# Null keys of the first wide attention: weights kept by token, scores scaled on GpSimd, the residual sum a tick later

## The reference, cut to what matters

```python
nkv = null_kv.reshape(HEADS, NUM_NULL_KV, 2, DIM_HEAD)
k = jnp.concatenate([nk, k], axis=2); v = jnp.concatenate([nv, v], axis=2)
q = _l2norm(q) * q_scale;  k = _l2norm(k) * k_scale
sim = jnp.einsum('bhid,bhjd->bhij', q, k) * ATTN_SCALE      # ATTN_SCALE = 8
sim = sim + dist * slopes                                    # alibi; then the causal mask
attn = jax.nn.softmax(sim, axis=-1)
out = jnp.einsum('bhij,bhjd->bhid', attn, v)
return out.transpose(0, 2, 1, 3).reshape(b, n, HEADS * DIM_HEAD) @ w_out
```

## Time and profile before

| | |
|---|---|
| median of 3 runs | 2622.32 us |
| the profiled execution | 2621.87 us |
| its span, first to last instruction | 2620.2 us |
| TensorE matmul busy | 2392.0 us (91%) |
| VectorE / ScalarE / GpSimd busy | 1722.9 (66%) / 1481.1 (57%) / 1605.7 us (61%) |
| mean granted TensorE clock | 0.968 |
| GpSimd's power in `pool_rstd` (L2593) | 256 times, mean 589 ns |
| GpSimd's power in the norm (L912) | 64 times, mean 2934 ns |

### The profile page before, as it was taken

One profiled execution on the slowest core, in us unless ns is written; L12 is line 12 of the kernel. 1 busy time (PEld: TensorE's weight loads), 2 busy tenths in 40 slices (PEclk: granted clock), 3 DMA queues, 4 the chain that ended last, 5 costly groups with the idle time before them and its releaser, 6 DMA issues. The chain is left out here.

```text
span 2620.2 us, 62757 instructions
## 1 busy us (share of the span) xinstructions
PE 2392.0 (91%) x24121; PEld 1873.6 (72%) x24121; DVE 1722.9 (66%) x4520; ACT 1481.1 (57%) x3071; POOL 1605.7 (61%) x2517
## 2 busy tenths in 40 slices
PE   4999999999998778888999999999999958789897
PEld 3888888888887556556777787787777748555555
DVE  4667677677775657785544467777777622477776
ACT  3666666666654457765444366666666523366665
POOL 4777777778786644443433267777777721566664
PEclk8999999999999969999999999999999979799999
DMA  3692000000000010000000000000000036000000
GB/s 115 205 331 84 2 2 2 2 2 2 2 2 1 1 53 2 2 2 1 23 1 1 3 2 6 6 4 6 6 6 4 6 116 190 17 8 10 8 4 33
DMA packets 23257, 83.12 MB, mean 32 GB/s; under 512 B 4113, under 2 KB 11026, under 8 KB 21938
## 3 DMA queue, kind: packets, MB, share of 16 engines
q1 hardware_dynamic: 19810, 71.90, 8.5%
q0 software_dynamic: 3152, 7.21, 0.9%
HBM read 71.89 MB, written 46.79 MB: 45 GB/s over the span
## 5 line engine op out<-in xcount | busy, mean ns | idle before, releaser
L891 POOL TENSOR_TENSOR XR<-XR,T 128x256 f32<-128x256 f32 x512 | 376.2, 735 | 151.9 <-DVE T L770 121.7
L645 ACT ACTIVATE P<-ps 128x384 f32<-128x384 f32 (+1 forms) x512 | 250.6, 542 | 177.4 <-PE ps L2575 176.0
L2575 PE MATMUL ps<-P,V 128*64 128x256 f32 (+3 forms) x4096 | 334.6, 348 | 7.0 <-DVE O L1396 5.2
L1380 DVE TENSOR_REDUCE bm<-ps 128x3 f32<-128x384 f32 x512 | 260.1, 550 | 100.5 <-PE ps L2575 99.8
L2575 PEld LDWEIGHTS ps<-P,V 128*64 128x64 f32 (+1 forms) x4096 | 186.3, 124 | 126.7 <-issue 32.2
L1305 ACT ACTIVATE P<-ps 128x768 f32<-128x768 f32 x256 | 207.7, 811 | 101.9 <-PE ps L2575 99.7
L781 DVE TENSOR_REDUCE sm<-ps 128x2 f32<-128x512 f32 (+1 forms) x256 | 130.8, 553 | 179.1 <-PE ps L2575 178.9
L1480 POOL TENSOR_SCALAR_AFFINE_SELECT P<-P 128x512 f32<-128x512 f32 x256 | 162.6, 635 | 124.3 <-ACT P L1305 122.4
L904 POOL TENSOR_TENSOR PS<-P 128x256 f32<-128x256 f32 x256 | 181.5, 734 | 69.5 <-ACT P L645 69.1
L2575 PE MATMUL ps<-mk,identb 128*128 128x256 bf16 (+1 forms) x1024 | 205.5, 296 | 17.2 <-DVE bm L1380 15.4
L912 POOL TENSOR_TENSOR ss<-ss,nhalf 128x16 f32<-128x16 f32 x64 | 187.8, 2934 | 5.3
(11 more groups left out here) (323 smaller groups left out, 7152.0 us busy)
## 6 DMA issues: line engine op xcount, KB each, us to landing
rows_i<-in_zero SPq DMA_DIRECT2D x16, 1208.0 KB, 32.0
rows_o<-in_zero SPq DMA_DIRECT2D x16, 1208.0 KB, 81.6
w<-in_m_w SPq DMA_DIRECT2D x23, 578.0 KB, 4.0
zt<-rows_i SPq DMA_DIRECT2D x23, 128.0 KB, 3.1
rows_o<-yo POOLq DMA_DIRECT2D x23, 128.0 KB, 3.7
stg<-in_t_w SPq DMA_DIRECT2D x11, 256.0 KB, 2.7
XR<-in_x SPq DMA_DIRECT2D x4, 512.0 KB, 8.4
out<-XR SPq DMA_DIRECT2D x8, 256.0 KB, 2.0
```

The costliest lines, as they stand in the source:

```text
L645: e.activation(self.P[at % 6][:, :], K.ps.ap("st", s, g, h)[:, 0:self.w], ACT.Exp, bias=0.0, scale=1.0 if kind == 0 else 0.125).then_inc(K ...
L891: p = po.e.tensor_tensor(x, x, self.T[g % 2][:, par, pr], ALU.add)
L1380: e.tensor_reduce(bm[:, h, :], K.ps.ap("mx", s, g, h)[:, 0:384].rearrange("p (a c) -> p a c", c=128), X, ALU.max, negate=True).then_inc(K. ...
L2575: return self.te.matmul(o, l, r, start=start, stop=True, skip_group_check=True)
```

## The change

Stage 0 alone is changed. The null keys' part leaves the products of each unit. GpSimd scales the null scores and adds the bias, right behind the norm (`pool_null`). It later adds the two exponentials of a head (`sm[:, 48:56]`), which VectorE adds to the transposed row sums before the reciprocal. In tick 22 GpSimd multiplies the exponentials by rs into pn, which is now one tile of 128 tokens by 64 for a whole sequence ("shared"). A new item "null" of each sequence starts when its last unit has ended: k = 0, TensorE transposes pn and ScalarE copies it into pnT; k = 1, TensorE multiplies pnT by nvw, "nul"; k = 2, VectorE adds nul to XR, after GpSimd's last sum. nvw, the null values times w_out, is made once, by eight matmuls and two copies in unit (0, 0). A unit has 24 ticks; its residual sum moves to the tick after "out", last in that tick (rank 7). Preps come last in a tick on VectorE. SP stages kb first and nvs, now one piece, last.

```diff
-            first, last, unit = 8, 9, 23
+            first, last, unit = 8, 9, 24
...
+            if kind == 0:
+                items.append((16 * b + first + 12 + unit, 2, "null", (b,), 3))
...
+        self.dve_order = [w for w in ticks(items, self.dve_rank) if not self.is_early(*w)]
...
     def done(self, b):
-        return self.summed, 4 * b + 4
+        return self.K.ps.read("nul", self.s, b) if self.kind == 0 else (self.summed, 4 * b + 4)
...
# rank
+        if name == "null":
+            return 3 if k == 0 else 2
# pool_rank
+        if name == "unit" and k == self.tk["out"] + 1:
+            return 7
+    def dve_rank(self, name, k):
+        return 6 if self.kind == 0 and name == "prep" else self.rank(name, k)
...
+    def pe_nvw(self, pe):
+        K, n = self.K, self.nvs_at
+        ps = K.ps.take(pe, self.G, "nvw")
+        K.staged(pe, n)
+        for j in range(8):
+            p = pe.e.matmul(ps[0:64, 0:128], K.stg[n % 2][:, 64 * j:64 * j + 64], K.wO[:, 128 * j:128 * j + 128],
+                            start=j == 0, stop=j == 7)
+        p.then_inc(K.ps.full_of("nvw"), 1)
+    def pe_null(self, pe, b, k):
+        K, s = self.K, self.s
+        if k == 0:
+            ps = K.ps.take(pe, self.G, "pnT", s, b)
+            pe.wait_ge(self.shared, 4 * b + 4)
+            K.tr(ps[0:64, 0:128], self.pn[b % 2][:, :]).then_inc(K.ps.full_of("pnT", s, b), 1)
+        if k == 1:
+            ps = K.ps.take(pe, self.G, "nul", s, b)
+            pe.wait_ge(self.nvs_in, 1)
+            pe.wait_ge(*K.ps.read("nvw"))
+            pe.wait_ge(*K.ps.read("pnT", s, b))
+            K.acc(ps[:, 0:256], self.pnT[b % 2][:, :], self.nvw[:, :], start=True).then_inc(K.ps.full_of("nul", s, b), 1)
...
# pe_unit, step mT
-            if kind == 0:
-                pe.wait_ge(self.pnull, g + 1)
-                for i in range(2):
-                    p = K.tr(ps[0:96, 256 + 128 * i:384 + 128 * i], fv(self.pn[g % 2][:, i, :]))
...
# pe_pv
-        if kind == 0:
-            pe.wait_ge(self.nvs_in, 4)
-            pe.wait_ge(*K.ps.read("mT", s, g))
-            for pr in range(2):
-                c = 256 * u + 128 * pr
-                K.acc(pv[:, 256 * pr:256 * pr + 256], self.nvs[:, 0, c:c + 128], self.pnT[g % 2][:, :], start=pr == 0)
-            K.acc(sm[:, 0:256], self.nvo[:, 4 * u:4 * u + 4, :].rearrange("p h c -> p (h c)"), self.pnT[g % 2][:, :],
-                  start=True)
...
# act_unit, step mT
-                i = e.activation(self.pnT[g % 2][:, :], ps[0:96, 256:512], ACT.Copy)
...
# dve
+            elif name == "null":
+                if k == 2:
+                    b = a[0]
+                    xs = K.XR[:, 2 * b:2 * b + 2, :].rearrange("p t c -> p (t c)")
+                    dv.wait_ge(self.summed, 4 * b + 4)
+                    dv.wait_ge(*K.ps.filled("nul", self.s, b))
+                    e.tensor_tensor(xs, K.ps.ap("nul", self.s, b)[:, 0:256], xs, ALU.add).then_inc(
+                        K.ps.out_of("nul", self.s, b), 1)
...
# dve_unit, step sT (kind 0)
+                if g >= 2:
+                    dv.wait_ge(self.shared, g - 1)
+                dv.wait_ge(self.pnull, g + 1)
...
+                dv.after(dv.step(e.tensor_tensor(rs[:, :], sums, self.sm[g % 4][:, 48:56], ALU.add)))
+            e.reciprocal(rs[:, :], rs[:, :] if kind == 0 else sums).then_inc(K.ps.out_of("sT", s, g), 1)
...
# dve_null: the four products and sums go, the reduction stays
+        dv.wait_ge(self.scored, g + 1)
...
# pool
-                if k == self.tk["out"] + (1 if self.kind == 2 else 0):
+                if k == self.tk["out"] + 1:
                     self.pool_sum(po, *a)
+    def pool_null(self, po, g):
...
+        po.wait_ge(*K.ps.read("sn", s, b))
+        if g >= 4:
+            po.wait_ge(self.rec, g - 3)
+        po.after(po.step(e.tensor_tensor(sn, snr, rq, ALU.mult)))
+        e.tensor_tensor(sn, sn, nb, ALU.add).then_inc(self.scored, 1)
...
# pool_unit: k == 3 ends with self.pool_null(po, g); k == 12 and k == 22:
+            ex = sm[:, 32:48].rearrange("p (a n) -> p a n", n=2)
+            e.tensor_tensor(sm[:, 48:56], ex[:, :, 0], ex[:, :, 1], ALU.add).then_inc(self.pnull, 1)
+        if k == self.tk["out"]:
...
+            po.wait_ge(*K.ps.read("sT", s, g))
+            e.tensor_tensor(
+                self.pn[b % 2][:, :].rearrange("p (t h n) -> p t h n", t=2, n=2)[:, :, 4 * u:4 * u + 4, :], ex,
+                self.rs[g % 2][:, :].rearrange("p (t h) -> p t h", t=2).unsqueeze(3).to_broadcast([128, 2, 4, 2]),
+                ALU.mult).then_inc(self.shared, 1)
```

More of the change, by code:

```diff
@@ L182, in __init__ @@
             self.sn = [sb(f"sn{s}_{i}", [128, 64], F32) for i in range(2)]
[L183 to L186, removed]
+            self.pn = [sb(f"pn{s}_{i}", [128, 64], F32) for i in range(2)]
+            self.pnT = [sb(f"pnT{s}_{i}", [64, 128], F32) for i in range(2)]
+            self.nvw = sb(f"nvw{s}", [64, 256], F32)
             self.on = sb(f"on{s}", [128, 128], F32R)
@@ L502, in pe_pv @@
                     p = K.acc(pv[64 * par:64 * par + 64, 256 * pr + q:256 * pr + q + w], V[:, kt, 2 * pr + par, :],
-                              P[2 * pr + par][:, c:c + w], start=kind == 2 and kt == 0 and pr == 0)
+                              P[2 * pr + par][:, c:c + w], start=kt == 0 and pr == 0)
         p.then_inc(K.ps.full_of("pv", s, g), 1)
@@ L507, in pe_pv @@
                 for h in range(4):
-                    p = K.acc(sm[32 * h:32 * h + 32, q:q + w], self.one[:, 0:32], P[h][:, c:c + w])
+                    p = K.acc(sm[32 * h:32 * h + 32, q:q + w], self.one[:, 0:32], P[h][:, c:c + w], start=kt == 0)
             p.then_inc(K.ps.full_of("sm", s, g), 1)
@@ L545, in act @@
                 a[0].act(ac, a[1], k)
+            elif name == "null":
+                if k == 0:
+                    b = a[0]
+                    if b >= 2:
+                        ac.wait_ge(*self.K.ps.filled("nul", self.s, b - 2))
+                    ac.wait_ge(*self.K.ps.filled("pnT", self.s, b))
+                    ac.e.activation(self.pnT[b % 2][:, :], self.K.ps.ap("pnT", self.s, b)[0:64, 0:128], ACT.Copy).then_inc(
+                        self.K.ps.out_of("pnT", self.s, b), 1)
             elif name == "unit":
@@ L548, in act @@
                     self.act_kb(ac)
+                if self.kind == 0 and a == (0, 0) and k == 8:
+                    self.act_nvw(ac)
                 self.act_unit(ac, *a, k)
@@ L565, in act_kb, with act_nvw @@
             e.activation(o, i, ACT.Copy).then_inc(self.kb_in, 1)
+    def act_nvw(self, ac):
+        K = self.K
+        ac.wait_ge(self.nv_zero, 1)
+        ac.wait_ge(*K.ps.filled("nvw"))
+        for t in range(2):
+            r = slice(32 * t, 32 * t + 32)
+            i = ac.e.activation(self.nvw[r, 128 * t:128 * t + 128], K.ps.ap("nvw")[r, 0:128], ACT.Copy)
+            i.then_inc(*((K.ps.out_of("nvw"), 1) if t else (self.nvs_in, 1)))
     def act_prep(self, ac, b, k):
@@ L670, in dve @@
                 K.ps.out_of("beff"), 1)
-        for name, a, k in self.order:
+        for name, a, k in self.dve_order:
             if name == "prep":
@@ L848, in pool @@
         if self.kind == 0:
-            for pn in self.pn:
-                e.memset(fv(pn[:, :, :]), 0.0).then_inc(K.pn_in, 1)
+            e.memset(self.nvw[:, :], 0.0).then_inc(self.nv_zero, 1)
         for name, a, k in self.pool_order:
@@ L935, in sp @@
         if self.kind == 0:
-            for n, (a, b) in enumerate(((0, 512), (512, 1024), (1024, 1040))):
-                n += self.nvs_at
-                K.sp_stage(sp, n, K.stg[n % 2][0:96, 0:b - a], K.t["nvs"][:, a:b])
             for c in range(5):
@@ L941, in sp @@
                 K.sp_stage(sp, n, K.stg[n % 2][:, 0:w], K.t["kb0"][:, 512 * c:512 * c + w])
+            K.sp_stage(sp, self.nvs_at, K.stg[self.nvs_at % 2][:, :], K.t["nvs"])
         else:
@@ L2840, in lay_out @@
     t["blk"] = blk
-    nv, no = np.zeros((96, 16, 64), f), np.zeros((96, 16), f)
+    nv = np.zeros((2, 64, 8, 2, 32), f)
     for h in range(16):
         for n in range(2):
-            for r in range(3):
-                at = 32 * r + 4 * (h % 2) + 2 * (h % 4 // 2) + n
-                nv[at, h], no[at, h] = nkv[h, n, 1], 1
-    t["nvs"] = np.concatenate([nv.reshape(96, 1024), no], 1)
+            nv[h % 2, :, h // 2, :, 2 * h + n] = nkv[h, n, 1][:, None]
+    t["nvs"] = nv.reshape(128, 512)
     t["wqT"] = np.ascontiguousarray(i["L0_attn_w_q"].T.reshape(8, 128, 128).transpose(1, 0, 2).reshape(128, 1024))
```

90 lines of the change are left out of this document (34 added, 56 removed).

## The result

The changed kernel takes 2667.39 us, median of 4 runs (2661.37 to 2671.27), beside 2623.86 for the kernel before on the same chip: ratio 1.0166, 95% interval 1.0140 to 1.0192. It is slower, by 43.5 us in the medians and by 39.5 us between the two profiled executions (2661.37 and 2621.87). The granted clock over the span fell from 0.968 to 0.961. The forecast was 2654 us in a range of 2622 to 2676.

The account below looks back on a forecast made before the run. TensorE, in program order, was taken to bound stage 0. Terms -39.7 + 12.8 + 39.9 + 19.6 + 2.5 - 3.0 + 0.5 = +32.6 on 2621.9 gave 2654 us, range 2622 to 2676.

Parts of the forecast that it names:

- The wait: TensorE before the query transposes (turn0): PSUM bank held until VectorE's add of nul, 2.85 us, 14 times, +39.9 us.
- The clock: TensorE after each such wait: half clock for 3.4 us, 1.4 us lost on average, 14 times, +19.6 us.
- Rival 1: TensorE in stage 0: the waits come but the clock stays whole, 2635 us; chance 0.18.
- The removed work: TensorE, each of 64 units: pn transposes, pnT products and pn wait go, 0.62 us a unit, -39.7 us.
- Work taken off it counts in full: TensorE in stage 0: as the bound, in program order, all removed work and every added wait counts in full.
- The added work: TensorE, each of 16 sequences: a pnT transpose, a float32 matmul and two row-count switches, 0.8 us, +12.8 us.
- Start: Start of stage 0: eight nvw products on TensorE before the first scores, behind the nvs transfer, +2.5 us.
- The accident: At 766 us: TensorE's 1.17 us idle and the half clock after it go, GpSimd's sum now behind the norm, -3.0 us.
- covered by 4 us: GpSimd's sum of a sequence's last unit ends at 329.0, 4 us before VectorE's add asks at 333; no cost.
- the end: End of stage 0: VectorE's last add follows GpSimd's last sum before the next stage may start, +0.5 us.
- Rival 2: TensorE in stage 0: the wait never forms as the add ends before Y; -26.9 us, 2595 us; chance 0.16.
- Rival 3: GpSimd in stage 0: raw 1 us late in 15 sequences, some half clock behind it, +18, 2672 us; chance 0.10.

Follow-up runs that it names:

- e1: Changed kernel with VectorE's add of nul first in its tick, ahead of the reductions: 2599.70 us, ratio 0.9916.
- e5: Changed kernel with VectorE's add of nul between the two T of its tick: 2644.31 us, ratio 1.0106.
- e2: Changed kernel with VectorE's add of nul behind the reductions but ahead of both T: 2623.33 us, ratio 1.0005.
- e12: Changed kernel with TensorE's nul moved behind sT in its tick, VectorE's order untouched: 2651.36 us, ratio 1.0122.
- e6: Changed kernel with the add first in its tick, minus the null item's three steps on all engines (output incomplete): 2578.42 us, ratio 0.9855.
- e4: Kernel before without the pn transposes, pnT copies and pnT products (null keys left out of the output): 2601.22 us, ratio 0.9918.
- e3: Kernel before with only the 24th tick and GpSimd's residual sum one tick later, last in it: 2616.82 us, ratio 0.9982.
- e7: Kernel before without TensorE's null-key transposes and products, and with VectorE's preps last in their tick: 2618.01 us, ratio 0.9992.
- e10: Changed kernel with add first in its tick and null item four ticks later, GpSimd's sum back ahead of the norm: 2642.65 us, ratio 1.0079.

## Why the prediction was right

**The wait.** Forecast: turn0 waits for VectorE's add of nul, eight takes further in the ring, 2.85 us late, 14 times. Found: 14 times, released by the add, and once more, which the forecast did not have: with no turn0 left, the bank of the last nul but one goes to nm, and TensorE waits 2.11 us at 856. By e1 stall and clock cost 4.37 us a sequence; with 1.6 for the clock (e5), 2.77 are the stall, 2.70 of them shown as idle. Term 39.9, measured 14 x 2.77 = 38.8, without the fifteenth. The add took 0.42 us, as its like in a later stage did, and the order on VectorE was as in the earlier trace rows. e1, e2 and e5 walk the add up that list, and the wait shrinks with every operation that it passes: 2.70, 2.10, 1.51, none. e12 shows that it is the ring.

**The clock.** The mechanism was right, the size low: 14 x 1.6 = 22.4, and some 2.5 for the two long stretches, for 19.6. The 24.9 lie just above the upper bound of 24. I had discounted for waits without it; among the 14 there were none. That is in part luck: 2.65 us in e12 and 2.45 us in e2 were followed by none, so the length of the gap does not settle it. Rival 1 asked for the clock to stay whole. It does at 1.51 us (e2) and not at 2.70. The Trainium skill (TensorE: Matmul & The Clock Gate, "HAM oscillation") warns only of gaps longer than either; the 0.58 of the changed kernel behind 2.70 us of idle time contradicts it, and giving the rows of before precedence was right.

**The removed work.** 0.62 us a unit forecast, 0.575 measured (e6): -36.8 for -39.7, still just under the lower bound of 0.58; which of its parts was worth less than its rows isn't shown. e4 shows that, taken out of the kernel before, it would not even have come in full, because VectorE's KL is late next. "Work taken off it counts in full" holds only as long as no other wait lies close behind.

**The added work.** 0.8 forecast, 0.84 measured (e6 against e1), from a shape that had no row: +13.4 for +12.8. Its parts (transpose, matmul, switches) were not measured one by one.

**Start.** +2.5 forecast; the first Y starts 1.2 us later (85.97 to 87.16), inside the bounds. It is no sharp measurement: in e2 and e5, which start as the changed kernel does, that Y stands at 85.96 and 88.66.

**The accident.** -3.0 forecast. The idle time of 1.17 us at 766 and the half clock behind it went, as the step says, but half of that came back: the changed kernel has 0.82 us before pn at 797, and a wait of 3.35 at 805 in place of 2.70, 1.5 us together. The first is set by GpSimd, the second by VectorE's small operations, held up beside GpSimd's sum; the forecast had that only as the upper bound of the stall (and put it down to GpSimd's multiplications; what runs beside L837 there is the sum). The sum, "covered by 4 us" in the forecast, ends 0.94 us before the add starts there (807.32, 808.26), so the cover is thin at the last sequences, but it held. Where the add stands first it does not: in e1 VectorE waits 4.33 us for that sum. e3 shows that the later sum alone only moves the accident to pn.

**The sum.** -36.8 + 13.4 + 38.8 + 22.4 + 2.5 + 1.2 - 3.0 + 1.5 = +40.0, against +39.5 between the profiled executions. Forecast +32.6. What was missing is the clock (5.3), the removed work (2.9), what came back of the accident (1.5) and 0.6 of added work, less 1.3 at the start, 1.1 of the stall and the 0.5 for the end, which no run measured by itself. That the sum comes so close is in part luck, since it leaves out three things. The fifteenth wait adds up to 2.1 us. The wait ahead of the next stage's first transposes is 1.0 us shorter (6.36 for 7.32). These start 40.9 us later than before (846.14 and 887.02), so 1.4 us are won back in stages that the change does not touch. The sequence came to 51.27 us and not to "some 50.5": 0.2 of that is the clock, 0.2 the removed work, and 0.4 my arithmetic, since the terms themselves give 48.36 - 2.48 + 0.8 + 2.85 + 1.4 = 50.9.

**Rival 2** was the right picture of another kernel. It asked that the add end before Y does; e1, which does that, takes 2599.70 where rival 2 gave 2595. **Rival 3** didn't come about in the changed kernel, where raw is never late, but the thin place that it rests on is real: e7 and e10 open it with one edit each, at 1.7 to 1.9 us a sequence.

## What to carry to other kernels

Where PSUM banks go round in one engine's program order, count the takes from each new product to the one that gets its bank back, and put the reader of the new product in the slowest engine's list: its place in that list, not its length, is the price (0.42 us of work cost 4.4 us a sequence here, and nothing a few places up). Price an idle gap of TensorE with what the clock does behind it, and take that from gaps of the same kernel. Work taken off the bounding engine counts up to the next wait only, so look for what is late next before it is counted in full.

## What the runs showed of the hardware

The half clock followed idle gaps of TensorE in an otherwise busy stretch the more often the longer they were, but length alone did not decide. Idle for 1.50 or 1.51 us: after none of 12 (e2). 1.69 to 1.74 us: after 4 of 14 in e7 and the one in e2, not after the one in e3. 1.89 us: after 9 of 14 (e10). 2.10 us: after 10 of 13 (e5; one of the 13 is 2.29 us). 2.12 us: after 9 of 13 (e12; one is 2.30). 2.45 us: after the one in e1, not after the one in e2. 2.65 us: not after the one in e12. 2.70 us and more: after all 14 in the changed kernel. But 1.17 us, with another short wait close behind it, was enough at 766 in the kernel before. Each short stretch of it (3.4 us) cost some 1.6 us beside the gap: sequences with it are 1.5 to 1.6 us longer than those without (e2, e5, e7, e10, e12). Gaps of one length in one kernel had it or not, so a forecast that counts them carries a scatter of some microseconds.

VectorE's small operations could take longer while GpSimd ran a residual sum: at 805 in the changed kernel nm 0.28 us for 0.17 and the two sm adds 0.78 for 0.24. Where VectorE's list is what TensorE waits for, that is 0.65 us of stall. It is not so for all of them: beside such a sum the two L837 took 0.66 us in the kernel before, the two L834 just ahead of them 0.23.
